# Mean embedding and projection: two weight loads more before the second user tile joins, with TensorE's share of its columns, the test for further rows, the bias loads and one list moved

## The reference

```python
valid = sequence_ids < emb_table.shape[0]              # (1024, 200), 12500 rows in the table
safe_ids = jnp.where(valid, sequence_ids, 0)
seq_emb = emb_table[safe_ids] * valid[..., None]       # rows of 512 float32
denom = jnp.maximum(valid.sum(axis=1, keepdims=True), 1.0)
user_repr = seq_emb.sum(axis=1) / denom                # (1024, 512)
logits = user_repr @ proj_w + proj_b                   # (1024, 12500)
```

## Time and profile before

| | us |
|---|---|
| median of 3 runs | 640.46 (640.25 to 640.85) |
| the profiled execution, whole time | 641.41 |
| its span, first to last instruction | 639.7 |
| TensorE matmuls busy | 609.9 (95%) |
| VectorE busy | 407.6 (64%) |
| GpSimd busy | 230.1 (36%) |
| ScalarE busy | 145.5 (23%) |
| last join (tile 7's transposes) | 355.15 |

### The profile page before, as it was taken

The page is one execution under the profiler, slowest core; times in us unless marked ns, Lnnn a source line. Parts: engine busy times, 40 slices in busy tenths (PEclk is TensorE's granted clock), DMA queues, the critical chain, the costliest instruction groups (busy, mean ns, idle before and its releaser), DMA issues.

```text
span 639.7 us, 7596 instructions
## 1 busy us (share of the span) xinstructions
PE 609.9 (95%) x2602; PEld 477.1 (75%) x2602; DVE 407.6 (64%) x723; ACT 145.5 (23%) x161; POOL 230.1 (36%) x227
## 2 busy tenths in 40 slices
PE   1989899999999999999999999999999999999997
PEld 0327558678787777788788788888888888888886
DVE  7988959989879698797785554332333333344442
ACT  8917525131140131300200221111011111211210
POOL 5777877767765667565550000000000000000000
PEclk9999999989999999999999999999999999999999
DMA  9989999989999889798793398454555555566632
GB/s 310 388 292 371 391 369 314 367 285 323 309 327 314 272 289 309 231 329 246 233 334 112 97 290 276 122 177 157 170 173 177 176 177 176 170 192 203 219 124 106
DMA packets 77703, 158.31 MB, mean 247 GB/s; under 512 B 9287, under 2 KB 65042, under 8 KB 77658
## 3 DMA queue, kind: packets, MB, share of 16 engines
q1 hardware_dynamic: 60378, 110.30, 51.0%
q0 software_dynamic: 17280, 47.47, 23.2%
HBM read 115.70 MB, written 51.20 MB: 261 GB/s over the span
## 4 chain that ended last, share of the span: by engine, by line
PE 76%; DVE 14%; issue 5%; DMA 3%; DVEq 1%; ACT 0%; POOL 0%; POOLq 0%
PE acc L829 72%; DVE sums L557 6%; DMA rows<-in_L_rec_emb_table_dram,index 3%; DVE w_lo L620 3%; PE turned L783 2%; DVE key L514 1%; DVE top L510 1%; PE turned L758 1%; PE acc L834 1%; PE turned L775 1%; DVE stage L635 1%; DVE mean L602 0%; POOL rows L349 0%; DVEq L255 0%; DMA ids_sb<-in_r_sequence_ids_dram 0%
## 5 line engine op out<-in xcount | busy, mean ns | idle before, releaser
L349 POOL DMA_INDIRECT rows<-in_L_rec_emb_table_dram,index x208 | 220.4, 1060 | 94.7 <-issue 57.0
L829 PE MATMUL acc<-w_hi,mean_hi 128*128 128x500 f32 x800 | 224.7, 402 | 0.8 <-ACT mean_hi L434 0.8
L635 DVE TENSOR_TENSOR stage<-acc,bias_sb 128x500 f32<-128x500 f32 x162 | 109.2, 676 | 181.8 <-PE acc L829 181.5
L829 PE MATMUL acc<-w_lo,mean_hi 128*128 128x500 f32 x800 | 214.7, 390 | 0.0
L829 PE MATMUL acc<-w_hi,mean_lo 128*128 128x500 f32 x800 | 214.3, 390 | 0.2 <-DVE mean_lo L607 0.2
L829 PEld LDWEIGHTS acc<-w_hi,mean_lo 128*128 128x128 f32 x800 | 150.7, 189 | 32.2 <-DVE mean_lo L607 1.2
L829 PEld LDWEIGHTS acc<-w_lo,mean_hi 128*128 128x128 f32 x800 | 150.8, 189 | 31.4
L829 PEld LDWEIGHTS acc<-w_hi,mean_hi 128*128 128x128 f32 x800 | 150.3, 189 | 32.0 <-issue 4.3
L557 DVE SCALAR_TENSOR_TENSOR sums<-rows,mask,sums 128x512 f32<-128x512 f32 x165 | 124.0, 752 | 8.2
L418 ACT ACTIVATE w_hi<-w_raw 128x2000 fp32r<-128x2000 f32 x39 | 72.9, 1875 | 232.6 <-PE acc L829 215.8
L620 DVE TENSOR_TENSOR w_lo<-w_raw,w_hi 128x1000 fp32r<-128x1000 f32 x74 | 85.2, 1193 | 10.5 <-ACT w_hi L418 10.5
(11 more groups left out here) (106 smaller groups left out, 180.4 us busy)
## 6 DMA issues: line engine op xcount, KB each, us to landing
out_dram<-stage SPq DMA_DIRECT2D x200, 250.0 KB, 3.7
w_raw<-in_L_rec_proj_w_dram SPq DMA_DIRECT2D x39, 1000.0 KB, 6.5
bias_sb<-in_L_rec_proj_b_dram SPq DMA_DIRECT2D x39, 250.0 KB, 4.6
raw_at_hi<-in_L_rec_proj_w_dram SPq DMA_DIRECT2D x4, 1000.0 KB, 10.1
rows<-in_L_rec_emb_table_dram,index POOLq DMA_INDIRECT x208, 5.8
raw_at_lo<-in_L_rec_proj_w_dram SPq DMA_DIRECT2D x3, 1000.0 KB, 14.3
stage<-in_L_rec_proj_w_dram SPq DMA_DIRECT2D x1, 1000.0 KB, 26.2
ids_sb<-in_r_sequence_ids_dram SPq DMA_DIRECT2D x1, 700.0 KB, 4.6
```

The source lines that it names most:

```text
L349: return pool.indirect_dma_start(out=dst, out_offset=None, in_=table, in_offset=bass.IndirectOffsetOnAxis(ap=column, axis=0), bounds_check ...
L635: dve.tensor_tensor(stage[:, g % STAGE, r - stores[g][0]], acc[:, r % BANKS, 0:BW], bias_sb[:, i % BIAS], ALU.add).then_inc(s_moved_by_dve, 1)
L829: last = nc.tensor.matmul(bank, first, second, start=part + k == 0, stop=part == 2 and k == K - 1 and not by_act[r])
```

## The change

It does seven things. (1) `JOIN` is (0, 12, 16, 19, 22, 24, 26, 28): tile 1 joins two loads later. There are now 49 loads, the joins stand at units 0, 12, 24, 37, 53, 67, 82 and 98, loads 5 to 12 are split at units 1 to 8, loads 13 to 16 at 13 to 16, 17 to 19 at 25 to 27, 20 to 22 at 38 to 40. `MORE_LOADS` stays 16. (2) `ON_PE` gives TensorE four columns of tile 1 (22 to 25) instead of eight; they are due at unit 10, their diagonals at unit number 9. (3) `DUE_FIRST`: tile 1's columns on VectorE are due in units 0 to 8. (4) `further_behind`: the test for further rows stands behind column 20 of its tile, and the wait for the last column goes into `mean_of`. (5) The four first bias loads stand at unit 3 (`BIAS_DUE`) and not among the first weight loads. (6) Tile 1's rest list is made behind tile 0's column 20 in a bank of its own (`LIST_FIRST_AT`), not behind unit 0; (7) two waits before unit 5 keep that bank. `GATHER_LEAD` is unchanged.

```diff
 def mean_embedding_projection(nc, ids, table, proj, bias, out, FAST=26,
-                              JOIN=(0, 10, 14, 17, 20, 22, 24, 26)):
+                              JOIN=(0, 12, 16, 19, 22, 24, 26, 28)):
     F32, F32R, BF16 = mybir.dt.float32, mybir.dt.float32r, mybir.dt.bfloat16
     I32, U32 = mybir.dt.int32, mybir.dt.uint32
     ALU, ACT, AX = mybir.AluOpType, mybir.ActivationFunctionType, mybir.AxisListType
...
     RAW, SPLIT, BIAS, ROWS, PLACED, BANKS = 2, 5, 4, 12, 2, 6
     CH = 2
-    ON_PE, DIAGS = ((0, FAST), (18, FAST), (24, FAST)), 4
+    ON_PE, DIAGS = ((0, FAST), (22, FAST), (24, FAST)), 4
     RAW_MORE, MORE_LOADS = 2, 16
+    FURTHER_BEHIND, LIST_FIRST_AT, BIAS_DUE = 20, 21, 3
     ACT_TILES, BOTH_TILES = 1, 5
     PART_AT = (0, 32, 64)
     BIAS_ROWS = PART_AT[-1] + NB
...
     dve_last = [max((c for c in range(FAST * t, FAST * (t + 1)) if not by_pe[c]), default=None) for t in range(TILES)]
     assert all(at % CH == 0 for pair in ON_PE for at in pair)
-    GATHER_LEAD = 5
+    further_behind = [min(FURTHER_BEHIND, pe_columns[t].start - 2) if pe_columns[t] else FURTHER_BEHIND
+                      for t in range(TILES)]
+    assert all(by_pe[FAST * t + j] is False and j >= FAST - ROWS for t, j in enumerate(further_behind) if t)
+    GATHER_LEAD, DUE_FIRST = 5, 8
     LATE_LOAD, REST_FIRST_AT, OPENED = 7, 18, SPLIT - 1
     def column_due(c):
...
         t, j = divmod(c, FAST)
         if by_pe[c]:
             return joined[t] - 2
-        begin, end = joined[t - 1] - 2 if t > 1 else 0, joined[t] - SUM_AHEAD
+        begin, end = (joined[t - 1] - 2, joined[t] - SUM_AHEAD) if t > 1 else (0, DUE_FIRST)
         return begin + (end - begin) * j // (dve_last[t] - FAST * t)
...
             return first_diags[c] if c < FAST else diag[:, nth[c] % DIAGS]
         def list_of(t):
-            return turned if t else first_list
+            return turned if t > 1 else first_list
         @block.sync
         def _(sp):
...
                 if q == LATE_LOAD:
                     sp.wait_ge(s_rows[(FAST - 1) % ROWS], 16 * ((FAST - 1) // ROWS + 1))
                 load_w(q)
-                if q == ONCE:
+            sp.wait_ge(s_bias_parts, 3)
+            for r in range(UNITS):
+                if r == BIAS_DUE:
                     for i in range(BIAS):
                         load_bias(i)
-            sp.wait_ge(s_bias_parts, 3)
-            for r in range(UNITS):
                 for g in range(len(stores)):
                     if stores[g][0] + stores[g][3] - 1 == r:
                         store(g)
...
             def sum_further(t):
                 if t:
-                    dve.wait_ge(s_summed, nth[dve_last[t]] + 1)
+                    dve.wait_ge(s_summed, nth[FAST * t + further_behind[t]] + 1)
                 else:
                     dve.memset(sums[:], 0.0).then_inc(s_cleared, 1)
                     dve.wait_ge(s_cleared, 1)
...
                                          ALU.add).then_inc(s_mean, 1)
             def mean_of(t):
+                dve.wait_ge(s_summed, nth[dve_last[t]] + 1)
                 dve.wait_ge(s_turned, t)
                 dve.wait_ge(s_rest_mean, t)
                 dve.scalar_tensor_tensor(mean[:], sums[:], inv_count[:, t:t + 1], rest_mean[:], ALU.mult,
...
                     if not by_pe[c] and column_due(c) == r and c >= FAST + 4:
                         add_column(c)
                         t, j = divmod(c, FAST)
+                        if j == further_behind[t]:
+                            sum_further(t)
                         if 1 < t and t + 1 < TILES and j in SORT_NEXT:
                             sort(t + 1, SORT_NEXT.index(j))
                         if t + 1 < TILES and j == (SELECT_NEXT if t > 1 else 15):
                             choose(t + 1)
                 for t in range(1, TILES):
-                    if r + MEAN_AHEAD == joined[t]:
-                        sum_further(t)
-                        if t >= len(ON_PE):
-                            mean_of(t)
+                    if t >= len(ON_PE) and r + MEAN_AHEAD == joined[t]:
+                        mean_of(t)
                 if r + TURN_AHEAD + 1 in joined[1:]:
                     mean_low(joined.index(r + TURN_AHEAD + 1))
...
             def list_rest(t):
                 pe.wait_ge(s_select, 2 * t + 2)
-                if t:
+                if t == 1:
+                    pe.wait_ge(s_placed, 1)
+                    pe.wait_ge(s_rest_index, 1)
+                elif t:
                     pe.wait_ge(s_mean_lo, t)
                 place_in = list_of(t)
                 nc.tensor.transpose(place_in[:, 0:P], select[:], ident[:])
...
             for c in pe_columns[0]:
                 if c == REST_FIRST_AT:
                     sum_rest(0)
+                if c == LIST_FIRST_AT:
+                    list_rest(1)
                 sum_column(c)
             turn(0)
             pe.wait_ge(s_bias_parts, 3)
...
                 q, t = units[r]
                 if r == 0:
                     pe.wait_ge(s_w_lo, OPENED)
+                if r == BANKS - 1:
+                    pe.wait_ge(s_placed, 2)
+                    pe.wait_ge(s_rest_index, 2)
                 if r == first_unit[q]:
                     pe.wait_ge(s_w_lo, q + 1)
                 if r >= BANKS:
...
                         first, second = ((hi, high), (hi, low), (lo, high))[part]
                         last = nc.tensor.matmul(bank, first, second, start=part + k == 0,
                                                 stop=part == 2 and k == K - 1 and not by_act[r])
-                if r in joined[:-1]:
+                if r and r in joined[:-1]:
                     list_rest(t + 1)
                 if by_act[r]:
                     last = nc.tensor.matmul(bank, pick[:, q % NB:q % NB + 1].to_broadcast([BIAS_ROWS, P]), bias_parts[:],
```

## The result

The changed kernel takes 650.94 us (median of 4 runs, 650.31 to 653.68) against 640.38 us for the kernel before on the same chip: 1.017 times as long, 95% interval 1.0159 to 1.0182. It is 10.6 us slower, where the forecast said 3.1 us and its range ended at 646.0. The profiled execution took 653.68 us with a span of 651.9.

The account below looks back on a forecast made before the run. TensorE, busy for 95% of the span, was taken to bound the kernel. The terms -5.44 + 5.6 + 2.5 + 0.3 + 1.9 - 1.75 gave +3.1 us on 640.46, so 643.6 us, range 638.1 to 646.0.

Parts of the forecast that it names:

- Two more units, -5.44: TensorE before the joins: two more units done by then, 2 x 2.72 = -5.44 us if joins kept their old times.
- Load 12 late, +5.6: Tile 1's diagonals on ScalarE wait for load 12, landing at 85.65; unit 10 at 91.8 against 86.22: +5.6 us.
- (a): SyncE's queue: four bias loads ahead of loads 11 and 12 delay load 12 by 5.2 us (0 to 5.2).
- (b): Start of the kernel: without bias loads, tile 0's last row lands earlier and releases load 7; 2.0 us gained (0 to 2.4).
- The clock, +2.5: TensorE behind the wait for tile 1's diagonals: eight column matmuls at half rate cost +2.5 us, 0 if the clock holds.
- its two supports: TensorE's earlier trace: column matmuls at 1075 and 622 ns after the initial idling; clock 0.51 for 3.5 us after 1.88 us idle.
- Tile 2, +0.3 (0 to 1.5): VectorE before tile 2's mean: load 16 goes out only after load 13's split, so its own split is +0.3 us late.
- Tile 3, +1.9 (0 to 3): VectorE before tile 3's mean: with two raw buffers load 19 waits for load 17's split, delaying the mean by +1.9 us.
- The clock at tile 3, 0: TensorE behind new waits for tile 3's mean: a second clock fall, left out of the sum.
- a rival with 1.7 us and a chance of 0.10: Slower still: waits for tile 3's mean lower the clock (1.7 us), tiles 6 and 7 give nothing; 647.1 us, chance 0.10.
- Tiles 6 and 7, -1.75: TensorE's waits for the means of tiles 6 and 7 (1.02 and 0.73 us) go with the test at column 20: -1.75 us.
- The rival in which the weights come in time: Load 12 lands before about 83, units resume at 86.22, VectorE's mean of tile 1 is +2.6 us late; 638.1 us, chance 0.20.

Follow-up runs that it names:

- the version that beats both: Changed kernel with the four bias loads at unit 5, tile 1's diagonals ahead of load 10's split, and MORE_LOADS at 20: 634.38 us, 0.9913 times before.
- the one with the old joins: Changed kernel with the joins of the kernel before, tile 1's eight columns on TensorE, DUE_FIRST = 7, bias loads at unit 5: 639.59 us, 0.9982 times before.

## Why the prediction was wrong

The direction and the places were right. The size was not, and the range ended 4.9 us too early. Four terms missed: when load 12 is issued, tile 2, tile 3, and the clock behind tile 3.

- **Two more units, -5.44: right.** A unit each is missing from the last two stages before the last join, 5.7 us together between the version that beats both and the one with the old joins. What is left of it as a gain is smaller, since tile 1 still comes later.
- **Load 12 late, +5.6: the time of its issue failed.** It landed at 88.7, not at 85.65, and TensorE's columns and unit 10 came 3.1 us behind the forecast with it. (a) The cost of the bias loads in front, +5.2, held: it made 12.1 + 5.2 = 17.3 us from issue to landing, and the trace has 17.5. That it fits so closely is luck, since the transfer took 16.6 to 20.1 us in the five kernels with the bias loads ahead and 11.5 to 12.8 in four that have them elsewhere. (b) The 2.0 us given back for the lighter start failed. With them load 12 would be issued at 68.35; it was issued at 71.19, which is 2.8 of the 3.1 us. Load 7 did go out 2.7 us earlier (43.40 against 46.09), but from load 9 on each load goes out behind a split on VectorE, in the order of its program. The split of load 5 ended at 59.09 and released load 9 at 59.12, no earlier than before (59.14). The lines of ScalarE and of VectorE show what held it: ScalarE made load 5's high half behind tile 1's rest list, for which it waited 4.13 us. VectorE had come to that list only at 53.32, behind its first columns of tile 1, whose rows weren't there before.

```profile
54.23 0.28 ACT L443 ACTIVATE placed<-acc 128x128 f32<-128x128 f32 x1 [4.13 <-DVE rest_index L583]
```

```profile
56.78 2.31 DVE L625 TENSOR_TENSOR w_lo<-w_raw,w_hi 128x1000 fp32r<-128x1000 f32 x2 [0.37 <-ACT w_hi L422]
```

Load 12 itself was issued at 71.19, against 70.35, since VectorE came to the split of load 8 only at 68.86, against 68.02. With the bias loads behind it, load 12 landed at 82.1, against 82.45 before: (b) was worth 0.3 us. I had let a gain pass through a chain (last row, load 7, load 12) without asking at each link what released it. The failed step is the "- 2.0" in "Load 12 then lands at 82.45 + 5.2 - 2.0".
- **The clock, +2.5: right** at that place (2.7 us between the two lengths of the same eight matmuls), though I had only picked it from between 1.7 and 3.3. One of its two supports wasn't one: in both windows of the earlier trace rows, 16.1 to 21.3 and 21.4 to 26.6, the profile has the granted clock at 1.00, so the 1075 and 622 ns there are no readings of a slow clock. The other, 3.5 us at 0.51, holds. The Trainium skill, page "TensorE: Matmul & The Clock Gate", section "Terms", puts the penalty at the throttled time times (1 - K/N), which for the 13.6 us above at half rate is 6.8 us; the trace doesn't agree, since TensorE was busy for only 5.32 us of them, and half of that is 2.7 us, what the columns lost.
- **Tile 2, +0.3 (0 to 1.5): too small.** The stage grew by 1.85 us; with load 16's buffer free earlier, 2.1 us of it went. VectorE began its split 11.3 us after the issue (113.44 to 124.75), where I had taken 8.2 from tile 4's group and had 10.2 to give, so it waited 1.0 us. The other 0.8 us is idle time of VectorE at the test (2.30 us against 1.49 before), and what lengthened that isn't shown.
- **Tile 3, +1.9 (0 to 3): the term that failed worst.** The stage grew by 4.7 us. I took 8.2 us from issue to split from tile 4's group. Here it was 155.60 to 167.37, 11.8 us. The difference is the transfer alone, load 19's after, and load 20's before, in the view of DMA issues:

```profile
w_raw<-in_L_rec_proj_w_dram SPq DMA_DIRECT2D x1, 1000.0 KB, 9.8
```

```profile
w_raw<-in_L_rec_proj_w_dram SPq DMA_DIRECT2D x1, 1000.0 KB, 6.2
```

The 3.6 us between them are more than the miss of 2.8. The failed step is "with a transfer 0.2 us slower 1.9". The 12.1 us of load 12 stood ready as a bound and weren't used for one.
- **The clock at tile 3, 0: left out of the sum.** I had it as a rival with 1.7 us and a chance of 0.10. In and behind the wait of 5.94 us it fell to 0.50, and that cost 2.4 us there. It depends on the term ahead of it: a wait that is underestimated also hides its clock.
- **Tiles 6 and 7, -1.75: right.** The waits went; alone the edit gave 1.35 us.

Taking the bias loads back to the start undoes (a) and (b), 3.2 us in the sum; the medians give 3.5. `MORE_LOADS` gives 7.2 with its clock, against 2.2 in the sum. By that the largest part of the miss is `MORE_LOADS`.

The rival in which the weights come in time got its condition in two kernels: load 12 was there by 82.97 and 82.20 with the bias loads at the start or at unit 9. What it foretold still didn't happen. The diagonals were late enough for TensorE to wait 5.61 and 4.35 us for them, the columns took 5.83 and 6.34 us, and unit 10 started at 91.0 and 90.8, not at 86.22. Only with early diagonals too does unit 10 start at 85.21, and then TensorE waits 2.66 us for VectorE's mean, as that rival said (2.6).

## What to carry to other kernels

Where a constant names a load or a step ("from load 16 on only two buffers"), it moves relative to everything when a schedule is shifted: look at each such constant first, and cost the loads that change sides. A transfer's time from issue to landing is a property of what is in the queues at that moment; take it from a row with the same traffic around it, and keep the longest seen as the bound. In front of an engine that works in order, place what others wait for ahead of what waits for a transfer, on every engine in the chain, since the second engine's wait hides behind the first.

## What the runs showed of the hardware

- With the DMA engines' share at 1.02 to 1.05 (372 to 395 GB/s), 1000 KB of bias, spread from rows of 2000 bytes over 128 partitions, lengthened the way of a load issued behind them from 11.7 to 17.5 us at the same issue time (71.19). Over the kernels with the later joins it is 11.5 to 12.8 us in four that have them elsewhere, 13.5 in the one that has them right behind the load, and 16.6 to 20.1 in the five that have them ahead; even from 12.8 to 16.6 the difference, 3.8 us, is more than the 2.6 us that 1000 KB take at 390 GB/s. Why it is more isn't shown: rows and stores share the engines at that time, and SyncE's own issues stretched to 2.5 and 3.8 us there, against 0.4 to 0.9 us where the bias loads came later. What stretched them wasn't tried.
- Extra matmuls in a wait kept the granted clock at 1.00 where it had been 0.50: 44 of them shortened the columns behind the wait by 2.7 us, 24 of them the stage behind by 1.8 us. The medians fell by 1.9 and 1.1 us, which with overlapping executions is little more than their noise.
- At half clock the same eight column matmuls took 6.33 us, at full clock 3.67. The clock was 0.50 for 6.7 us in and behind the wait of 5.94 us, and 0.51 for 3.5 us behind that of 1.88 us in the kernel before. Behind that of 2.10 us ahead of tile 1's columns it stayed at 1.00, and so it did in the kernel after behind a wait of 2.30 us for tile 2's mean. So the length of the last wait alone doesn't say whether the clock falls; what does wasn't settled.
